# A graph network's edge phases on one Trainium2 core: odd chunks of the relational phases gather three of eight tiles on TensorE, even chunks four

## The reference, cut to what matters

```
x += L0(h)   # messages h[src] times a 16x16 matrix made from edge_attr_16, summed at dst; batch norm; relu
x += L1(h)   # m = silu(einsum(h[dst], edge_attr_8, W)) @ W_lin, summed at src; gated update
x += L2(h)   # relational, two layers (l2a, l2b):
             #   msg = h[src] @ W[edge_type];  norm = 1 / max(count[dst, edge_type], 1)
             #   out = segment_sum(msg * norm, dst) + h @ root + bias;  relu between, log_softmax at the end
x += L3(h)   # x[src] scaled by out-degree, summed at dst, scaled by in-degree
```

## Time and profile before

| | us |
|---|---|
| median of 3 runs (4679.73 to 4683.43) | 4680.27 |
| the profiled execution | 4656.31 |
| its span, first to last instruction | 4654.4 |
| PE busy | 4430.5 (95%) |
| DVE busy | 4185.4 (90%) |
| POOL busy | 3395.2 (73%) |
| ACT busy | 3232.3 (69%) |
| mean granted TensorE clock | 0.981 of full |

### The profile page before, as it was taken

The page is one execution under the profiler, slowest core; times in us unless marked ns, Lnnn a source line. Parts: engine busy times, 40 slices in busy tenths (PEclk is TensorE's granted clock), DMA queues, the critical chain, the costliest instruction groups (busy, mean ns, idle before and its releaser), DMA issues.

```text
span 4654.4 us, 106164 instructions
## 1 busy us (share of the span) xinstructions
PE 4430.5 (95%) x29576; PEld 3072.3 (66%) x29576; DVE 4185.4 (90%) x11965; ACT 3232.3 (69%) x5459; POOL 3395.2 (73%) x2615
## 2 busy tenths in 40 slices
PE   4999999999997999999988999999999999799998
PEld 3677777777774444444436777776777777566665
DVE  5999999999997999999987999997999999789887
ACT  4777777777774666666645777775777777577776
POOL 4888888888874888888845767665767676587886
PEclk8999999999997999999999999999999999899999
DMA  2111111111112222222212111111111111111111
GB/s 68 20 18 18 17 18 18 18 17 18 18 16 54 57 58 57 58 58 57 58 33 42 27 27 27 27 27 37 27 27 27 27 27 27 26 31 31 31 31 24
DMA packets 344557, 152.04 MB, mean 33 GB/s; under 512 B 268541, under 2 KB 329033, under 8 KB 344393
## 3 DMA queue, kind: packets, MB, share of 16 engines
q0 software_dynamic: 112000, 66.23, 10.5%
q1 hardware_dynamic: 232517, 85.33, 7.4%
HBM read 138.72 MB, written 9.77 MB: 32 GB/s over the span
## 4 chain that ended last, share of the span: by engine, by line
PE 79%; DVE 9%; issue 5%; DMA 3%; ACT 1%; POOL 1%; SPq 1%; DVEq 0%; POOLq 0%; ACTq 0%
PE acc L599 37%; PE rows_ps L756 15%; PE bank L692 13%; PE bank L772 4%; PE bank L764 2%; PE counts L606 2%; PE rows_ps L680 2%; DMA fields_all<-table_l,row_numbers 2%; DVE raw L1443 1%; PE counts L603 1%; PE eaT_ps L668 1%; POOL fields_all L583 1%; DVE stationary L1236 1%; DVE raw L1260 1%; DVE one_hot L1208 1%
## 5 line engine op out<-in xcount | busy, mean ns | idle before, releaser
L599 PE MATMUL acc<-one_hot,stationary 125*128 125x392 bf16 x12000 | 2343.7, 330 | 54.6 <-issue 28.3
L583 POOL DMA_INDIRECT gathered<-table_l,row_numbers x1200 | 1599.9, 1333 | 464.2 <-issue 356.0
L599 PEld LDWEIGHTS acc<-one_hot,stationary 125*128 125x128 bf16 x12000 | 1109.1, 99 | 755.3 <-issue 135.6
L867 ACT ACTIVATE distances<-count_hi,fields 125x392 bf16<-125x392 f16 (+1 forms) x2500 | 1222.5, 557 | 0.0
L1236 DVE TENSOR_TENSOR stationary<-mask,parts 125x1024 bf16<-125x1024 bf16 x1500 | 945.1, 684 | 0.2 <-ACT mask L852 0.2
L583 POOL DMA_INDIRECT fields_all<-table_l,row_numbers x600 | 765.9, 1277 | 237.8 <-issue 152.2
L852 ACT CAST mask<-is_lo 125x1024 bf16<-125x1024 f32 x500 | 521.7, 1043 | 460.1 <-issue 302.5
L1208 DVE TENSOR_SCALAR one_hot<-count_hi,fields 125x392 bf16<-125x392 f16 x2300 | 728.9, 342 | 13.5 <-issue 13.5
L692 PE MATMUL bank<-w,h1T 128*125 128x256 f32 x3200 | 717.2, 382 | 12.0 <-DVE product L1253 9.0
L583 POOL DMA_INDIRECT gathered<-table_l2a,row_numbers x400 | 511.4, 1279 | 288.3 <-DVE parts L1218 124.5
L756 PE MATMUL rows_ps<-node_parts,h1T 125*125 125x192 bf16 (+1 forms) x7200 | 679.4, 252 | 26.7 <-DVE node_parts L1287 19.5
(11 more groups left out here) (212 smaller groups left out, 4046.8 us busy)
## 6 DMA issues: line engine op xcount, KB each, us to landing
near_key<-near_keys_by_chunk SPq DMA_DIRECT2D x300, 122.1 KB
gathered<-table_l,row_numbers POOLq DMA_INDIRECT x1200
fields<-edge_fields SPq DMA_DIRECT2D x500, 31.2 KB
fields_all<-table_l,row_numbers POOLq DMA_INDIRECT x600
gathered<-table_l2a,row_numbers POOLq DMA_INDIRECT x400
gathered<-table_l2b,row_numbers POOLq DMA_INDIRECT x400
ea<-in_edge_attr SPq DMA_DIRECT2D x100, 62.5 KB
near_key<-near_keys_by_chunk SPq DMA_DIRECT2D x100, 61.0 KB
```

Of the source, the lines that this page charges most:

```text
L583: pool.indirect_dma_start(out=gathered[ph][:, s, t, :], in_=table[ph], out_offset=None, in_offset=bass.IndirectOffsetOnAxis(ap=row_numbers ...
L599: mm = pe.matmul(acc[:, :], stationary[:, s, k, t, :, :].rearrange("p a b -> p (a b)"), one_hot[:, s, t, :], start=first and t == 0 and k ...
L867: ins = act.activation(distances[:, i * n:(i + 1) * n], count_hi[:, 0:n], ACT.Abs, scale=-1.0, bias=fields[:, s, k, t:t + 1].bitcast(F32))
```

## The change

The number of near tiles becomes a pair, one for each slot; in l2a and l2b it is 4 for even chunks and 3 for odd ones. Odd chunks have five far tiles (0 to 4) and three near ones (5 to 7). All that counted by phase now counts by phase and slot: the waits, the loops and the widths of the near operations. The counts of l0, l1 and l3 stay. The diff, cut to its core (`far(ph)` became `far(ph, s)` and `NEAR_OF[ph]` became `NEAR_OF[ph][s]` in all other places too, where the waits, loops and slices of the same form are):

```diff
-NEAR_OF = {"l0": 0, "l1": 2, "l2a": 4, "l2b": 4, "l3": 4}
+NEAR_OF = {"l0": (0, 0), "l1": (2, 2), "l2a": (4, 3), "l2b": (4, 3), "l3": (4, 4)}
 NEARS = 4
-NEAR1 = NEAR_OF["l1"]
+NEAR1 = max(NEAR_OF["l1"])
...
-        def far(ph):
+        def far(ph, s):
-            return T - NEAR_OF[ph]
+            return T - NEAR_OF[ph][s]
...
-        def keys_of(ph):
-            return slice(NEARS, KEYS) if ph == "l1" else slice(0, NEARS)
+        def keys_of(ph, s):
+            end = KEYS if ph == "l1" else NEARS
+            return slice(end - NEAR_OF[ph][s], end)
...
-                    sp.wait_ge(S[ph]["rows_in"][s], 16 * far(ph) * pair)
+                    sp.wait_ge(S[ph]["rows_in"][s], 16 * far(ph, s) * pair)
...
-                n, at = NEAR_OF[ph] * EP, keys_of(ph).start * EP
+                n, at = NEAR_OF[ph][s] * EP, keys_of(ph, s).start * EP
...
-                    for t in range(far(ph)):
+                    for t in range(far(ph, s)):
                         pool.indirect_dma_start(
...
-            def near_rows(ph, chunk):
+            def near_rows(ph, chunk, s):
...
-                for t in range(NEAR_OF[ph]):
+                for t in range(NEAR_OF[ph][s]):
                     for g, (first, end) in enumerate(((0, NEAR_LO), (NEAR_LO, BLOCK))):
...
                     if ph != "l3" and follows(chunk, 2):
-                        near_turn(ph, chunk + 2)
+                        near_turn(ph, chunk + 2, s)
                     add_chunk(ph, chunk, s, range(4, 6))
                     if ph != "l3" and follows(chunk, 3):
-                        near_rows(ph, chunk + 3)
+                        near_rows(ph, chunk + 3, 1 - s)
...
-                act.copy(near_outerT[:, 0:NEAR_OF[ph] * EP], bank[TURNED_BANK][:, 0:NEAR_OF[ph] * EP]).then_inc(near_copied, 1)
+                act.copy(near_outerT[:, 0:NEAR_OF[ph][s] * EP], bank[TURNED_BANK][:, 0:NEAR_OF[ph][s] * EP]).then_inc(near_copied, 1)
...
-                n = NEAR_OF[ph]
+                n = NEAR_OF[ph][s]
                 number = (near_type1 if ph == "l1" else near_type)[:, bass.ds(chunk, 1), :].rearrange("p c j -> p (c j)")
+                number = number[:, number.shape[1] - n:]
...
-                count, before_this = NEAR_OF[ph], chunks_before(ph) + chunk
-                rows = near_rows_ps[ph]
+                count, before_this = NEAR_OF[ph][s], chunks_before(ph) + chunk
+                rows = near_rows_ps[ph][:, 0:count]
...
-                    n = far(ph)
+                    n = far(ph, s)
                     dve.wait_ge(near_done, chunks_before(ph) + chunk + 1)
```

More of the change, by code:

```diff
@@ L759, in near_rows, with near_turn @@
                 mm.then_inc(near_gathered, 1)
-            def near_turn(ph, chunk):
+            def near_turn(ph, chunk, s):
                 pe.wait_ge(near_outers, chunks_before(ph) + chunk + 1)
-                for t in range(NEAR_OF[ph]):
+                for t in range(NEAR_OF[ph][s]):
                     mm = pe.transpose(bank[TURNED_BANK][:, t * EP:(t + 1) * EP],
@@ L967, in silus @@
                 act.wait_ge(near_done, chunks_before("l1") + chunk + 1)
-                act.activation(msg[:, s, far("l1"):T, :],
+                act.activation(msg[:, s, far("l1", s):T, :],
                                bank[MESSAGE_BANK[s]][0:EP, 0:NEAR1 * F].rearrange("p (t f) -> p t f", t=NEAR1),
@@ L971, in silus, with near_copy @@
                 act.wait_ge(S["l1"]["step"], done("l1", "raw", chunk))
-                act.activation(msg[:, s, 0:far("l1")], raw[:, s, 0:far("l1")], ACT.Silu, scale=scale).then_inc(silu_ready, 1)
-            def near_copy(ph, chunk):
+                act.activation(msg[:, s, 0:far("l1", s)], raw[:, s, 0:far("l1", s)], ACT.Silu, scale=scale).then_inc(silu_ready, 1)
+            def near_copy(ph, chunk, s):
                 act.wait_ge(near_turned, chunks_before(ph) + chunk + 1)
@@ L986, in near_bits_of @@
                     act.wait_ge(near_picked, chunks_before(ph) + chunk - 1)
-                bits = near_bits[:, bass.ds(chunk, 1), keys_of(ph)].rearrange("p c k -> p (c k)")
-                act.copy(near_bits_now[:, s, 0:NEAR_OF[ph]].bitcast(I8), bits.bitcast(I8)).then_inc(near_bits_in, 1)
+                bits = near_bits[:, bass.ds(chunk, 1), keys_of(ph, s)].rearrange("p c k -> p (c k)")
+                act.copy(near_bits_now[:, s, 0:NEAR_OF[ph][s]].bitcast(I8), bits.bitcast(I8)).then_inc(near_bits_in, 1)
             def near_place(chunk, s):
                 act.wait_ge(near_picked, chunks_before("l3") + chunk + 1)
-                act.copy(gathered2[:, s, far("l3"):T, :], near_rows_ps["l3"][:, :, 0, :]).then_inc(ev("l3_near_placed"), 1)
+                act.copy(gathered2[:, s, far("l3", s):T, :], near_rows_ps["l3"][:, 0:NEAR_OF["l3"][s], 0, :]).then_inc(ev("l3_near_placed"), 1)
             def masks_and_near(ph):
@@ L999, in near_result @@
                     else:
-                        near_copy(ph, chunk)
+                        near_copy(ph, chunk, s)
                 near_bits_of(ph, 0, 0)
@@ L1295, in near_begin @@
             def near_begin(ph, chunk, pair, s, groups=(0, 1)):
-                n = NEAR_OF[ph] * EP
+                n = NEAR_OF[ph][s] * EP
                 for g in groups:
@@ L1340, in near_finish @@
                 if ph != "l3":
-                    near_types(ph, chunk)
+                    near_types(ph, chunk, s)
                 dve.wait_ge(near_halved, HALVINGS * before_this + 3)
@@ L1366, in near_finish @@
                     dve.wait_ge(near_counted, 3 * chunk + 3)
-                    dve.reciprocal(edge_norm[:, bass.ds(chunk * T + far("l1"), NEAR1)], near_count[:])
+                    dve.reciprocal(edge_norm[:, bass.ds(chunk * T + far("l1", s), NEAR1)], near_count[:])
             def begin_chunk(ph, chunk, pair, s):
@@ L1442, in l1 @@
                 dve.wait_ge(ev("l1_products"), chunk + 1)
-                st.mark(dve.tensor_reduce(raw[:, s, 0:far("l1")], product1[:, 0:far("l1")].rearrange("p t (j h) -> p t h j", h=F), AX.X, ALU.add))
+                st.mark(dve.tensor_reduce(raw[:, s, 0:far("l1", s)], product1[:, 0:far("l1", s)].rearrange("p t (j h) -> p t h j", h=F), AX.X, ALU.add))
                 st.mark(matches(is_type[:], count_lo, s, TYPE, RELATIONS))
@@ L1451, in edge_norms @@
                         st.wait("typed")
-                        st.mark(dve.tensor_tensor(is_type[:, 0:far("l1")], is_type[:, 0:far("l1")], gathered1[:, s, 0:far("l1"), RELATIONS * F:], ALU.mult))
+                        st.mark(dve.tensor_tensor(is_type[:, 0:far("l1", s)], is_type[:, 0:far("l1", s)], gathered1[:, s, 0:far("l1", s), RELATIONS * F:], ALU.mult))
                     if k == 1:
                         st.wait("weighed")
-                        st.mark(dve.tensor_reduce(edge_norm[:, bass.ds(chunk * T, far("l1"))], is_type[:, 0:far("l1")], AX.X, ALU.add))
+                        st.mark(dve.tensor_reduce(edge_norm[:, bass.ds(chunk * T, far("l1", s))], is_type[:, 0:far("l1", s)], AX.X, ALU.add))
                 split(st, msg[:, s], edge_norms)
@@ L1543, in l3 @@
                 one_hots("l3", s, (0, 1))
-                dve.wait_ge(S["l3"]["rows_in"][s], 16 * far("l3") * (pair + 1))
+                dve.wait_ge(S["l3"]["rows_in"][s], 16 * far("l3", s) * (pair + 1))
                 dve.wait_ge(ev("l3_near_placed"), chunk + 1)
```

24 lines of the change are left out of this document (12 added, 12 removed).

## The result

The changed kernel takes 4736.44 us (median of 4 runs, 4728.75 to 4738.86) against 4680.09 for the kernel before (4 runs): a ratio of 1.0119, 95% interval 1.0107 to 1.0131. It is slower by 56 us; I had forecast 26 less. Its profiled execution took 4738.86 us, with a span of 4737.0.

The account below looks back on a forecast made before the run. TensorE bounds l2 before, GpSimd after: 450 gathers at 1.59 us (715.5) plus start and end terms finish a phase at 3194.8 instead of 3207.8, 13.0 us less, 26 for both: 4680.3 - 26 = 4654 us, range 4622 to 4691.

Parts of the forecast that it names:

- TensorE's term: Row matmuls, transpose and message matmuls of one tile leave each odd l2 chunk: 0.82 us a pair, 82 us in all.
- GpSimd's term: Nine gathers a pair of l2 chunks at 1.59 us, 14.31 us a pair: GpSimd becomes the bound, phase 13.0 us shorter.
- the gaps without waits: Sign in l2: GpSimd's gaps all 0.30 us after the first chunks, with no 1.3 us wait for VectorE.
- one sign that I had named: Sign in l2: VectorE waits for gathered rows at the message step, which carries GpSimd's pace to the end.
- 13.5 us a pair: VectorE's need in l2 after narrower operations save at least 0.23 us a pair; below TensorE's 13.68 by little.
- The loop of rows, selection and transposes: TensorE's rows, VectorE's selection and outer product, TensorE's transposes in l2: 0.26 us left, costing 0 to 0.2 us a pair.
- My last sentence: Forecast wrong if gathers come under 1.57 or over 1.62 us, or VectorE's waits add up to over 14.5 us a pair.
- (c): Rival: VectorE's stationary writes delay one gather of every l2 chunk by 0.60 us; 24 us slower, 4704; chance 0.15.
- break-even 1.619 us: Cost of one l2 gather with its gap at which the change gains nothing, 728.5 / 450.
- The rule of the Trainium skill that I had weighed: VectorE in a two-port mode blocks GpSimd's descriptor writes until it ends; the l2 trace showed only 0.28 us of delay.

Follow-up runs that it names:

- both_three: Changed kernel with three near tiles and five gathers in every chunk of l2a and l2b, chip 5: 4773.99 us, 1.0264 of before.
- no_fifth: Changed kernel without its added gather, so four gathers in odd chunks too (wrong result), chip 6: 4558.92 us, 0.9819 of before.
- late_before: Kernel before with the near-rows signal of l2a and l2b sent some 1.2 us late: 4770.28 us, ratio 1.0261.
- one_gather: Changed kernel with a single gather a chunk in l2a and l2b (wrong result), chip 15: 4584.44 us, 0.9804 of before.
- late_close: Changed kernel with transposes moved behind two more tiles of sums and l2's near-rows signal some 1.2 us late, chip 5: 4689.10 us, 1.0078 of before.
- gpsimd_fills: Changed kernel with one gather a chunk in l2 and a GpSimd fill of scratch memory for each gather left out, chip 8: 4915.71 us, 1.0589 of before.
- after_fifth: Changed kernel unchanged, run again as control on chip 8: 4619.00 us, 0.9957 of before.
- before_again: Kernel before, unchanged, profiled once more on chip 6: 4642.83 us, ratio 1.0001.

## Why the prediction was wrong

**What bounds the kernel, and TensorE's term: right.** 0.82 us of TensorE in each odd chunk was put at 82 us; taking only that gave 83.4.

**GpSimd's term: the number right, the mechanism only in part.** Nine gathers at 1.59 us were foretold, 1.588 measured on chip 8, and the gaps without waits, TensorE idle 26 us a phase (forecast 0.4 to 0.6 us a pair, 20 to 30) and VectorE nearly full came as written. A phase was to be 13.0 us shorter and is 12.4 (724.5 in the mean of both on chip 8, 736.8 for before on chip 6), and the whole is 21.8, 24.0 and 27.4 us shorter on chips 5, 8 and 6 (forecast 26). But one sign that I had named did not come: VectorE waiting for gathered rows at the message step. It stands in the list of `both_three`, ten gathers a pair, and not in that of chip 8. There VectorE reads a chunk's rows 5.3 us after its last gather has ended (median of l2a, from the events; 1.6 in `both_three`), and GpSimd comes back to a slot that has been free for 1.9 us. So neither waits for the other. What is full beside GpSimd is VectorE: I had put it at 13.5 us a pair, and it is busy 13.9; `no_fifth`, with the same work of VectorE and eight gathers, needs 13.3. The difference is in operations that gathers lengthen (last section), and TensorE waits for VectorE's outer product (43.1 us in the list of chip 8). That the two keep one pace because each holds the other is my reading and not shown. That nine times the price of a gather gave the time to 1 us a phase is in part luck.

**The loop of rows, selection and transposes: the step that failed.** I wrote that 0.26 us is left there and that this "may cost between 0 and 0.2 us a pair, which makes TensorE's pair 13.7 to 13.9". That took TensorE's signal as prompt. On the first chip every third signal of l2 comes over 0.8 us late, 0.78 us in the mean over all, and a phase takes 764 us in place of 724: 0.8 us a pair more, about 15.1 where 14.3 was forecast. Neither TensorE, VectorE nor GpSimd is full then; each waits in turn. My last sentence named this outcome ("if VectorE's waits for GpSimd and for TensorE add up, so that a pair is over 14.5 us though GpSimd has gaps"), but I gave it no price and no chance: no rival held it.

**The rival on the other side, (c): right sign, wrong mechanism.** It had the gathers dearer, from VectorE's stationary writes in a fixed place, break-even 1.619 us. The gathers were 1.268 us long on the first chip, not longer, and the mean gather of an l2 phase is 1.22 to 1.29 us in every run here, before its gap of 0.30. The fixed place does exist; on chip 8:

```profile
2903.66 1.89 DVE L1237 TENSOR_TENSOR stationary<-mask,parts 125x1024 bf16<-125x1024 bf16 x3
2903.69 1.74 POOL L584 DMA_INDIRECT gathered<-table_l2a,row_numbers  x1 [0.30 <-issue]
```

A gather that starts with the first write takes 1.73 us, once a pair, and one that starts 1.0 us after it 1.35, once a pair. The other seven take 1.21, so the mean is 1.28, the same as in the kernel before with one of 1.49 in four. The rule of the Trainium skill that I had weighed (SBUF — State Buffer, section "SBUF: two separate sides") is told of VectorE's operations in a two-port mode, and the same section says that `tensor_tensor`, which the stationary writes are, has no such mode: it was not the rule for them. The trace shows that they delay a gather all the same, by 0.53 us at most, less than one write of 0.684.

**Why the changed kernel and not before.** This is argued, not shown. One reading is lost room: before has 93 us a phase of GpSimd's waits and 43 of VectorE's to take up a delay, and the change spends both. `late_before` speaks against it as the whole: the same delay of 1.2 us costs before 61 us a phase and the changed kernel 35, though before has more of this room. The other reading is that signals are held more often with nine gathers in the loop. Mild lateness doesn't decide either: in two executions alike in l3 (19 and 21 signals late), the mean in l2 is 0.14 and 0.12 us in before and 0.09 and 0.14 in the changed kernel on chip 6, and both lose 1 to 4 us a phase against their prompt lengths. A profile of before on a chip like 15 would tell; none was taken.

**What I could have read.** Three things stood in the profile. VectorE's wait for rows was 30.4 us in 82 chunks, 0.37 each, at one of the places where TensorE hands over work. l3, where the gathers are GpSimd's steady work and TensorE isn't full, had 19 late signals. And the profiled execution, which was none of the timed ones, was 24.0 us quicker than the median; I carried that as a constant, where the timed runs lived in a condition which the profile hardly showed, whose cost was at least 24 us in before and unknown in the change.

## What to carry to other kernels

When a change takes the slack out of a loop that crosses engines three or four times, price the hand-overs too: list each signal in the loop, see how late it comes in the stretch of the trace where GpSimd gathers without rest, and ask what the loop costs if each is 1 us later (here 73 and 120 us for one of them, 1.2 us late). A gap between the profiled execution and the median is not an offset to add but a condition to identify. When a time comes out as forecast, look for the wait that was to produce it: on chip 8 it was missing. And a gain of 0.5% that rests on one chip wants a second chip before it is believed, in either direction.

## What the runs showed of the hardware

**TensorE's completion signals can be held while GpSimd issues gathers.** Late signals (over 0.3 us behind the modelled end) arrive nearly all at two places of a gather, counted over the whole execution by the time since the start of the last gather (us; 6, 7 and 241 signals of the three rows come later than 1.65):

```
                              0.00-0.45  0.45-0.75  0.75-1.20  1.20-1.65
after, first chip: late            0        123          0        374
after, chip 15: late               0         90          0        345
before, chip 6: all signals      415        372        486        890
```

A gather's own record is 1.21 us, so three in four are released just after one ends; on a chip with prompt signals they fall anywhere. Together with `one_gather` this ties the lateness to gathers. But gathers alone don't make it: in l0, where GpSimd gathers eight tiles a chunk without rest, 3 of 894 signals are over 0.8 us late on the first chip and 2 of 946 on chip 15. The end of a matmul is modelled, so by this alone it could be TensorE that is slow rather than its signal; against that stands that the sums behind the rows start at 2617.76, 3.90 us before the rows' signal. Yet TensorE isn't undisturbed: the next sums come in twos, with gaps that no recorded wait explains.

```profile
2618.49 0.49 PE L600 MATMUL acc<-one_hot,stationary 125*128 125x392 bf16 x2 [0.24 <-issue]
2619.26 0.49 PE L600 MATMUL acc<-one_hot,stationary 125*128 125x392 bf16 x2 [0.27 <-issue]
```

The Trainium skill (Perfetto Trace Analysis, section "Tensor Engine Instruction (MATMUL, LD_WEIGHTS)") says that the profiler estimates a matmul's end, and that the semaphore moves only when PSUM has acknowledged the write. The trace agrees that the two can differ, by 0.01 us as a rule and by 3.7 in the stretch above; which part of the path is held, no run here shows. Nor is it settled why chips or sessions differ: chips 5, 6 and 8 had 0 to 19 late signals in an l2 phase of the changed kernel, chip 15 and the first chip 124 to 137. The order of the work counts too: `late_close`, on chip 5, had 71 and 59.

**A VectorE operation can wait out GpSimd's fills, and gathers too.** In `gpsimd_fills`, groups of VectorE over 2600 to 3200 us, and the same two in `after_fifth` below:

```profile
L1246 DVE TENSOR_TENSOR stationary<-mask,parts 125x1024 bf16<-125x1024 bf16 x209 | 131.6, 684 | 0.0
...
L1312 DVE TENSOR_SCALAR h1T<-near_key,node_key 125x500 bf16<-125x500 f16 x69 | 121.0, 1754 | 0.0
```

```profile
L1237 DVE TENSOR_TENSOR stationary<-mask,parts 125x1024 bf16<-125x1024 bf16 x246 | 154.9, 685 | 0.0
...
L1303 DVE TENSOR_SCALAR h1T<-near_key,node_key 125x500 bf16<-125x500 f16 x80 | 27.5, 345 | 4.8 <-DMA near_key<-near_keys_by_chunk 4.8
```

and the timeline of one chunk of it, GpSimd's fills and the comparison beside them:

```profile
2720.27 3.39 POOL L596 MEMSET scratch<- 125x1280 bf16 x3
```

```profile
2721.93 1.85 DVE L1312 TENSOR_SCALAR h1T<-near_key,node_key 125x375 bf16<-125x375 f16 x1
```

The comparison shown ends (2723.78) just after the fills do (2723.66), whole train and all. The mean of 1754 is of two kinds: 34 of 69 take 0.34 us and 35 take 3.05 to 4.17. The stationary writes, 684, do not feel the fills. The Trainium skill (SBUF — State Buffer, section "SBUF: two separate sides") says that of GpSimd and a VectorE operation in a two-port mode the one that starts first holds the shared ports for its whole length and the other is blocked. The trace agrees for these fills.

It agrees for gathers, too. In `after_fifth` the second cast of the split takes twice the 227 ns that it takes in the kernel before, and the timeline shows one beside its gather (before, `after_fifth`, and two rows of the timeline of `after_fifth`):

```profile
L1224 DVE CAST parts<-rest 125x128 bf16<-125x128 f32 x82 | 18.6, 227 | 2.8
...
L1225 DVE CAST parts<-rest 125x128 bf16<-125x128 f32 x82 | 37.4, 456 | 2.8
...
2916.48 1.21 POOL L584 DMA_INDIRECT gathered<-table_l2a,row_numbers  x1 [0.30 <-DVE parts L1219]
2917.06 0.65 DVE L1225 CAST parts<-rest 125x128 bf16<-125x128 f32 x1
```

From 2470 to 3170 us, 47 of 98 such casts, 100 of 392 one-hots and 47 of 194 key comparisons are longer than the rest, and 83 of 193 key comparisons in `before_again` (mean there 455 ns, up to 736). Every one of them starts 0.5 to 0.9 us after a gather and ends 1.2 to 1.4 us after its start, as the gather's record of 1.21 us ends. That is also where three in four late signals come; whether the two have one cause, no run here shows. The stationary writes stay at 685. A fill is no stand-in for a gather all the same: it holds VectorE for up to 4 us, and the l2 phases of 875 and 872 us say nothing on the change.
